# Quantizing the rotated y of a feed-forward stage: from token-major with transposes of z to channel-major, with maxima and factors carried by TensorE

## The reference, cut to what matters

```
def act_quant(x):                      # per token
    scale = 127.0 / clip(max(abs(x), axis=-1), 1e-5)
    return clip(round(x * scale), -128, 127) / scale

def h_bitlinear(x, w):
    xq = act_quant(fwht(x))            # Walsh-Hadamard transform along the channels
    return einsum('bsh,oh->bso', xq, weight_quant(w))    # weights -1, 0, 1 times a scale

gate = h_bitlinear(x, w_gate)          # 512 -> 2048
up   = h_bitlinear(x, w_up)            # 512 -> 2048
out  = h_bitlinear(silu(gate) * up, w_down)              # 2048 -> 512
```

## Time and profile before

| | |
|---|---|
| median of 3 runs | 3168.82 us (3165.68 to 3171.07) |
| the profiled execution's own time | 3169.14 us |
| its span | 3166.6 us |
| busy, share of the span | TensorE 87%, weight loads 46%, VectorE 63%, ScalarE 45%, GpSimd 32% |
| the feed-forward stage's loop | from about 2571.6 to 3077.2 us, 26 turns |

### The profile page before, as it was taken

How to read it: one execution, slowest core, us unless ns; L and a number is a source line. 1 busy time by engine, 2 the same in 40 slices (tenths; PEclk the granted TensorE clock), 3 DMA queues, 4 the chain that set the end, 5 groups by cost and what they waited for, 6 DMA issues and landing times. The chain is left out here.

```text
span 3166.6 us, 66615 instructions
## 1 busy us (share of the span) xinstructions
PE 2769.1 (87%) x26934; PEld 1468.4 (46%) x26968; DVE 1992.6 (63%) x2992; ACT 1438.4 (45%) x2378; POOL 1009.6 (32%) x712
## 2 busy tenths in 40 slices
PE   6999999387888888988845899999999799999997
PEld 2444444142444444444423444444444366666664
DVE  3444444359889898898891544445443377777776
ACT  2222222275667767757622422222222255666664
POOL 0000000108438347265390000000000077777776
PEclk9999999687898989889866999999999899999998
DMA  6999898300000000000002232322220101111110
GB/s 233 334 334 328 287 325 313 113 6 9 2 29 2 29 13 18 28 9 22 15 15 94 85 107 80 107 93 81 79 80 27 61 31 40 40 43 40 40 43 30
DMA packets 126427, 290.25 MB, mean 92 GB/s; under 512 B 30496, under 2 KB 35360, under 8 KB 122112
## 3 DMA queue, kind: packets, MB, share of 16 engines
q1 hardware_dynamic: 122752, 261.91, 23.7%
q10 hardware_dynamic: 3456, 25.17, 2.4%
HBM read 245.02 MB, written 42.01 MB: 91 GB/s over the span
## 5 line engine op out<-in xcount | busy, mean ns | idle before, releaser
L814 POOL TENSOR_TENSOR b_tmp<-b_L,b_U 128x496 f32<-128x496 f32 (+30 forms) x248 | 253.3, 1021 | 501.9 <-ACT b_L L1058 483.0
L2020 POOL TENSOR_TENSOR d_zb<-d_za 128x1024 f32<-128x1024 f32 x32 | 75.4, 2355 | 1007.6 <-DVE d_za L2082 1007.6
L860 PE MATMUL b_e<-b_hT,b_wqkv 128*128 128x512 f16 x1152 | 284.0, 393 | 46.4 <-DVE b_raw L1250 36.3
L1300 DVE TENSOR_TENSOR b_U<-b_U,b_tmp 128x1488 f32<-128x1488 f32 (+30 forms) x248 | 282.5, 1139 | 8.6
L816 POOL TENSOR_TENSOR b_U<-b_U,b_tmp 128x496 f32<-128x496 f32 (+30 forms) x248 | 274.3, 1106 | 19.4
L1298 DVE TENSOR_TENSOR b_tmp<-b_L,b_U 128x1488 f32<-128x1488 f32 (+30 forms) x248 | 264.9, 1068 | 17.4 <-ACT b_L L1058 11.8
L1526 PE MATMUL c_r<-c_hT,c_g_pair 128*128 128x512 f16 x1056 | 253.5, 392 | 13.1 <-DVE c_hT L1691 13.1
L1700 DVE SCALAR_TENSOR_TENSOR c_av<-c_r,c_sg 128x512 f32<-128x512 f32 x88 | 60.8, 691 | 303.0 <-PE c_r L1526 246.4
L1887 PE MATMUL d_m<-s_region,d_xiT 128*128 128x512 bf16 x1021 | 237.5, 384 | 6.2 <-ACT d_xiT L2000 2.2
L1526 PE MATMUL c_r<-c_hT,c_u_pair 128*128 128x512 f16 x1056 | 242.7, 379 | 0.0
L1526 PE MATMUL c_d<-c_d_pair,c_aT 128*128 128x512 f16 x1056 | 241.0, 379 | 0.0
(11 more groups left out here) (236 smaller groups left out, 5524.8 us busy)
## 6 DMA issues: line engine op xcount, KB each, us to landing
a_cT<-in_ctxT SPq DMA_DIRECT2D x128, 512.0 KB, 9.7
a_cn<-in_ctx SPq DMA_DIRECT2D x128, 512.0 KB, 8.9
a_x_ln<-in_x SPq DMA_DIRECT2D x8, 1024.0 KB, 16.2
a_cw<-in_ctx SPq DMA_DIRECT2D x128, 64.0 KB, 9.5
a_x_res<-in_x SPq DMA_DIRECT2D x32, 256.0 KB, 10.8
x<-a_x_out SPq DMA_DIRECT2D x32, 256.0 KB, 10.7
b_xg<-x SPq DMA_DIRECT2D x8, 1024.0 KB, 5.5
om<-b_hT SPq DMA_DIRECT2D x32, 256.0 KB, 2.0
```

The lines of the kernel that those rows point to most:

```text
L814: nc.gpsimd.tensor_tensor(tmp[:, QV, s + 1:S, :], lo, us, ALU.mult).then_inc(pool_prod, 1)
L860: mm = pe.matmul(p[:], w_qkv[:, a, i, n, c * P:(c + 1) * P], hp[:, b, n, :], start=(n + a + b == 0), stop=(n == DC - 1 and a == 1))
L1300: V.tensor_tensor(U[:, 0:QV, s + 1:S, :], U[:, 0:QV, s + 1:S, :], tmp[:, 0:QV, s + 1:S, :], ALU.subtract).then_inc(sub, 1)
L2020: nc.gpsimd.tensor_tensor(o[:, :, 0, :], a[:, :, 0, :], a[:, :, 1, :], ALU.add).then_inc(bf, 1)
```

## The change: what it does, and the diff

`rotate_y` swaps the operands: `had1` is stationary, and the four transposed chunks, 512 columns, are streamed. z comes out with channels on the partitions and (chunk, token) along the free axis, which is the form that the down projection wants, so the 16 transposes of z, their copies and the tile `zq` go.

Tokens now lie on the free axis, so the factor has to be found and applied otherwise:
- VectorE takes, for each channel-in-chunk and token, the largest magnitude over the 16 chunks (`largest`: `zm`, 128 x 128, read through a view whose inner step is 128 elements).
- TensorE transposes `zm` (`turn_largest`, between the gates 1 and 2), and VectorE reduces it to one number per token, from which the factor is worked out as before, and made a diagonal matrix (`factor`, after the second y).
- TensorE multiplies a matrix of ones with the diagonal (`spread_factor`, after the gates), which puts each token's factor on all partitions, and VectorE multiplies z with it, 2 x 1024 elements (`scaled`, after the fourth y).
- ScalarE adds the large constant and takes it off again in two passes for each half (`whole_z`), the second writing `ziT` in bf16. The clip goes.

The ring `RQ` now holds `largest`, `factor`, `down` and `pad`. `largest` and `down` share a bank, so the transpose of `zm` waits for `d_x_out`. GpSimd's last level waits for the product instead of ScalarE's passes.

```
-                    for c in range(4):
-                        mm = pe.matmul(p[:, c * P:(c + 1) * P], yT[:, 4 * j + c, :], had1, start=True, stop=True)
-                    mm.then_inc(full, 1)
+                    pe.matmul(p[:], had1, yT[:, 4 * j:4 * j + 4, :].rearrange("p c n -> p (c n)"),
+                              start=True, stop=True).then_inc(full, 1)
...
+            def turn_largest(i):
+                p, full = RQ.open(pe, i, "largest")
+                pe.wait_ge(zm_ready, i + 1)
+                pe.transpose(p[:, 0:P], zm[:], ident[:]).then_inc(full, 1)
+
+            def spread_factor(i):
+                p, full = RQ.open(pe, i, "factor")
+                pe.wait_ge(diag_ready, i + 1)
+                pe.matmul(p[:, 0:P], ones[:], diag[:], start=True, stop=True).then_inc(full, 1)
...
+            def whole_z(i, h):
+                act.wait_ge(zs_ready, 2 * i + h + 1)
+                half = slice(h * W // 2, (h + 1) * W // 2)
+                A.activation(zs[:, half], zs[:, half], ACT.Identity, bias=offset[:, 0:1]).then_inc(whole, 1)
+                act.wait_ge(whole, 2 * i + h + 1)
+                if h == 0 and not (isinstance(i, int) and i == 0):
+                    RQ.take(act, i - 1, "down")
+                part = ziT[:, WC // 2 * h:WC // 2 * (h + 1), :]
+                A.activation(part.rearrange("p c n -> p (c n)"), zs[:, half], ACT.Identity, bias=offset[:, 1:2])\
+                    .then_inc(zi_ready, 1)
...
+            def scaled(i):
+                dve.wait_ge(zi_ready, 2 * i)
+                p, free = RQ.take(dve, i, "factor")
+                for h in range(2):
+                    half = slice(h * W // 2, (h + 1) * W // 2)
+                    ins = V.tensor_tensor(zs[:, half].rearrange("p (c n) -> p c n", n=P),
+                                          z[:, half].rearrange("p (c n) -> p c n", n=P),
+                                          p[:, 0:P].unsqueeze(1).to_broadcast([P, WC // 2, P]), ALU.mult)
+                    ins.then_inc(zs_ready, 1)
+                dve.wait_ge(zs_ready, 2 * i + 2)
+                dve.sem_inc(free, 1)
...
+            def largest(i):
                 dve.wait_ge(bf, 6 * (i + 1))
-                V.tensor_reduce(amax2[:], z[:], AXX, ALU.max, apply_absolute_value=True).then_inc(am2, 1)
+                V.tensor_reduce(zm[:], z[:].rearrange("p (c n) -> p n c", n=P), AXX, ALU.max,
+                                apply_absolute_value=True).then_inc(zm_ready, 1)
+
+            def factor(i):
+                p, free = RQ.take(dve, i, "largest")
+                V.tensor_reduce(amax2[:], p[:, 0:P], AXX, ALU.max).then_inc(am2, 1)
                 dve.wait_ge(am2, 3 * i + 1)
+                dve.sem_inc(free, 1)
...
+                dve.wait_ge(q2, i + 1)
+                V.tensor_scalar(diag[:], ident[:], fac2[:, 0:1], None, ALU.mult).then_inc(diag_ready, 1)
```

More of the change, by code:

```diff
@@ L1805, in ffn_phase @@
         za, zb, z, zs = (sb(n, [P, W]) for n in ("za", "zb", "z", "zs"))
-        zq = sb("zq", [P, W], BF16)
+        zm, diag, ones = (sb(n, [P, P]) for n in ("zm", "diag", "ones"))
         amax2, step2, inv2, fac2, dsc = (sb(n, [P, 1]) for n in ("amax2", "step2", "inv2", "fac2", "dsc"))
@@ L1812, in ffn_phase @@
                   [f"z{j}" for j in range(NB)], 4, "m")
-        RQ = Ring(st, ["zi0", "zi1", "down", "pad"], 2, "q")
+        RQ = Ring(st, ["largest", "factor", "down", "pad"], 2, "q")
         set_ready = sem("set")
@@ L1816, in ffn_phase @@
         xT_hi, am, q1, xs_ready, clip1 = (sem(n) for n in ("xT_hi", "am", "q1", "xs_ready", "clip1"))
-        y_ready, zo_ready, first, bf, am2, q2, zs_ready, clip2 = (
-            sem(n) for n in ("y_ready", "zo_ready", "first", "bf", "am2", "q2", "zs_ready", "clip2"))
+        y_ready, zo_ready, first, bf, am2, q2, zs_ready = (
+            sem(n) for n in ("y_ready", "zo_ready", "first", "bf", "am2", "q2", "zs_ready"))
         dsc_ready, summed = sem("dsc"), sem("summed")
+        zm_ready, diag_ready, whole, zi_ready = (sem(n) for n in ("zm_ready", "diag_ready", "whole", "zi_ready"))
         def steps(eng, body):
@@ L1879, in transpose_xi, with gates @@
                 mm.then_inc(full, 1)
-            def gates(i, r):
-                RX.used(pe, r - 1, "xiT")
-                for j in range(NB):
+            def gates(i, r, js):
+                if js[0] == 0:
+                    RX.used(pe, r - 1, "xiT")
+                for j in js:
                     for n, w in (("g", w_g), ("u", w_u)):
@@ L1927, in body @@
                 if do["main"]:
-                    gates(k, r)
+                    gates(k, r, (0, 1))
+                if do["end"]:
+                    turn_largest(k - 2)
+                if do["main"]:
+                    gates(k, r, (2, 3))
+                if do["end"]:
+                    spread_factor(k - 2)
                 if do["one"]:
@@ L1938, in body @@
                     transpose_y(k)
-                if do["end"]:
-                    transpose_zi(k - 2, 0)
                 if do["main"]:
[L1942 to L1946, removed]
+                    rotate_y(k, range(NB))
                 if do["one"]:
@@ L1984, in body @@
                         A.copy(yT[:, 4 * j:4 * j + 4, :].rearrange("p c n -> p (c n)"), p[:]).then_inc(free, 1)
+                if do["end"]:
+                    whole_z(i, 0)
                 if do["one"]:
@@ L1989, in body @@
                 for h in range(2):
[L1990 to L1993, removed]
+                    if do["end"] and h == 0:
+                        whole_z(i, 1)
                     if do["main"]:
@@ L2029, in _ @@
             V = nc.vector
-            V.memset(offset[:], MAGIC).then_inc(set_ready, 1)
+            V.memset(offset[:, 0:1], MAGIC)
+            V.memset(offset[:, 1:2], -MAGIC).then_inc(set_ready, 1)
+            V.memset(ones[:], 1.0).then_inc(set_ready, 1)
             V.tensor_copy(ident16[:], ident[:]).then_inc(set_ready, 1)
@@ L2115, in body @@
                         gated(k, j)
-                    if do["end"] and j == 2:
-                        clip_z(i, 0)
+                    if do["end"] and j == 1:
+                        factor(i)
+                        V.tensor_scalar(dsc[:], step2[:], wscale[:, 2:3], 1.0 / QMAX, ALU.mult, ALU.mult)\
+                            .then_inc(dsc_ready, 1)
+                if do["end"]:
+                    scaled(i)
                 if do["two"]:
                     low_xT(k + 2, r)
-                if do["end"]:
-                    clip_z(i, 1)
                 if do["one"]:
```

33 lines of the change are left out of this document (5 added, 28 removed).

## The result

The changed kernel takes 3299.9 us (median of 4 runs, 3296.94 to 3302.22), the kernel before beside it 3167.25 (3163.13 to 3171.07): a ratio of 1.0419, 95% interval 1.0401 to 1.0437. The forecast was 3263 with a range up to 3300. The profiled execution took 3300.22, its span 3298.4 us.

The account below looks back on a forecast made before the run. TensorE bounds the kernel at 19.44 us a turn; the new loop of waits takes 21.81 plus 0.8 for the clock, 3.17 more over 29 intervals, 92 us, plus 2 at the end: 3169 + 94 = 3263 us, range 3200 to 3300.

Parts of the forecast that it names:

- closed row: Feed-forward loop: waits from ScalarE's `d_xT` to the next close a loop of 18.51 + R us, 21.81 a turn, over TensorE's 18.49.
- ScalarE's pairs: ScalarE between y's copies and `d_zo`: two dependent pairs of added passes, 2.04 us a pair, 4.08 a turn.
- my own case: Whole kernel: the stride costs VectorE time and the clock falls now and then; 3240 to 3290 us, chance 0.55.
- the list: Start-to-start steps of one turn across ScalarE, VectorE and TensorE, 21.81 us in sum, plus 0.8 for the clock.
- R: VectorE's strided reduction over z: its time, taken as 3.3 us, the middle between 2.29 and 4.28.
- 5.57 + 0.64 + 0.8: TensorE: `zm` transpose, gates, spread and rotation of x 5.57 us; x's transposes until `d_xT` 0.64; clock 0.8.
- The clock: TensorE behind the new gap: granted clock falls, costing 1.58 us, in half of the turns, so 0.8 a turn.
- A small reduction, a diagonal, all off the chain: VectorE's added products, small reduction and diagonal were to be off the chain; the products about 1.22 us each.
- The new wait: TensorE idles 2.3 us at the transpose of `zm`, whose bank `d_x_out` frees behind VectorE's strided reduction.
- One sign: Expected in the profile after: ScalarE's `d_zo` 4 us later behind y's copies than in the kernel before.
- TensorE's 18.49: TensorE's work in a turn of the changed loop without waits: 18.49 us, against 19.44 a turn before.
- Rival 3: Feed-forward loop: TensorE stays the bound, a turn is 0.95 us shorter, 3141 us in all; chance 0.05.

Follow-up runs that it names:

- Experiments 1: Changed kernel with the reduction over z reading 16 neighbours contiguously, the maxima taken over other elements: 3226.76 us, 1.0181 of the kernel before.
- experiment 4: Changed kernel with ScalarE's second pair of passes moved behind both `d_zo` and the copy of xi: 3237.22 us, 1.0218 of the kernel before.
- experiment 2: Changed kernel with 11 unused matmuls of 384 columns on TensorE ahead of the wait for `zm`: 3291.47 us, 1.0395 of the kernel before.
- experiment 5: Changed kernel with the diagonal written by ScalarE between its second and third silu, not by VectorE: 3260.85 us, 1.0292 of the kernel before.
- experiment 3: Changed kernel with maxima and down projection on separate banks and `d_x_out` behind the factor: 3296.59 us, 1.0397 of the kernel before.
- experiment 9: Version with passes and down projection one turn later and diagonal by ScalarE, its silus, passes and bank pad reordered: 3147.94 us, 0.9934 of the kernel before.
- experiment 7: Changed kernel with passes and down projection one turn later, z in two buffers, other banks, diagonal by ScalarE: 3185.69 us, 1.0058 of the kernel before.
- experiment 10: Changed kernel with VectorE's diagonal as a three-operand SCALAR_TENSOR_TENSOR in place of TENSOR_SCALAR: 3300.04 us, 1.0411 of the kernel before.

## Why the prediction was right, and where its terms were off

- **The mechanism** was the one forecast: a closed row through ScalarE's pairs, butterfly, reduction, `d_x_out`, gates and x's transposes, longer than TensorE's own work. Experiments 1 and 4 took one member each out, and the turn fell by nearly its length (4) or by more (1). Nearly all of the loss is in these turns: from the first reduction to the last are 598.7 us before and 727.8 after, 129 of 131 us. Behind the last one are 4.1 us more, forecast 2, and ahead of the first 1.3 less.
- **That the range held is luck.** 3299.9 is 0.1 us inside its end, with single runs on either side (3296.94 to 3302.22), and above the 3240 to 3290 of my own case. The kernel became 133 us slower, forecast 94.
- **The sum was short by 1.45 us a turn.** Along the list, from `d_xT` at 2824.06 to the next at 2848.12 are 24.06, forecast 21.81 + 0.8. The pairs took 2.37 and 2.22, not 2.04 twice: +0.51; a pass took 1.14 to 1.19, not the 1.06 of the earlier trace rows. From reduction to TensorE's transpose 4.54, not R + 1.00 = 4.30: +0.24. From the transpose to `d_xT` 7.78 in this turn, one with a fall of the clock, not 5.57 + 0.64 + 0.8: +0.77. The rest agrees within 0.07 in sum. The mean turn is 23.94, so 1.33 short, and 29 of these are 39 us: all that the forecast lacks. The row taken for a pass, line 1082 of the kernel, is a silu without a bias operand, the new passes have one; whether that makes the 0.1 us, no run shows.
- **R** is 3.69 in this turn. My 3.3, a middle between 2.29 and 4.28, was too low. The Trainium skill's figure ("Vector Engine (DVE) Microarchitecture Reference", section "Measured stream behaviour on trn2"), by which I had given an estimated 3.6 to 3.7, agrees with the trace. The single-source case that the same section reports at the full rate, a stream that alternates between two regions, did not carry over to this reduction.
- **The clock** fell in 17 of 26 turns, forecast half of them, and cost TensorE 1.4 to 1.7 us each time, forecast 1.58. But experiment 2 shows what that was worth to the turn: 0.34 us on average, forecast 0.8.
- **"A small reduction, a diagonal, all off the chain"** is the step that failed. From `d_x_out` there are two routes to the spread of the factor: TensorE's gates, at full clock 4.6 us (0.93 to the transpose, 0.2 for it, 3.46), and VectorE's y, y, factor, diagonal, 5.44 (2839.41 to 2844.85). The second is the longer one once the clock is whole. An error of 1 us here stood beside one on the clock with the other sign. The diagonal was long because of GpSimd: 0.40 us by ScalarE (experiment 5) gave 1.0 us a turn.
- **The new wait** was at the place forecast, 2.0 to 2.5 us (forecast 2.3), released by `d_x_out`. But taking the shared bank away gave nothing (experiment 3), because the diagonal held the spread at the same place; the bank is not shown to cost anything by itself.
- **One sign failed.** `d_zo` was to start 4 us later behind y's copies. It starts 7.15 us behind the first of them (2824.56 to 2831.71), before 4.91 (2815.58 to 2820.49), so 2.24 later: in the earlier trace rows a copy of `ziT` and 1.29 us of waiting stood in the pairs' place. The list itself had it right. Silu no longer waits for `d_fac`, as forecast.
- **TensorE's 18.49** and the rotation in 3.60 (forecast 3.61) held; experiment 9 runs at it. Rival 3, TensorE as the bound and 3141 us, is what that version comes near (3148), with the passes among the silus, where the prediction had said that they cost nothing.

## What to carry to other kernels

Work moved from an idle stretch of an engine to one that closes a loop between engines costs nearly its whole length (1.94 of 2.22 us a turn in experiment 4), though the engine's busy time hardly changes (in the loop's 26 turns ScalarE was busy 307.45 us before and 306.74 after). Two routes that run beside each other hide each other's cost: taking away one (the clock in experiment 2, the bank in experiment 3) shows next to nothing, and tells only that there is another. A small VectorE instruction beside GpSimd's work is as long as GpSimd leaves it: look at where it ends, not only at its length. When a change shortens the bound engine's work but lengthens such a loop, putting the tail a turn later is worth trying before tuning its members: here one pair moved gave 63 us (experiment 4), the later tail with its other changes 152 (experiment 9).

## What the hardware showed that I had not expected

- VectorE instructions of 128 or 512 columns with all their tensors in SBUF ended with GpSimd's running instruction: the diagonal 0.08 us after it in each turn of the loop, `d_xq` 0.28 after it in experiment 5. The diagonal took 0.29 us at least, 1.41 in the median and up to 2.01, in experiment 3 up to 2.43; `d_xq` took 0.43 in the median in experiment 7 and 1.48 in experiment 5. The kernel before had it too: its `d_zq` passes (line 2065, 1024 columns) took 1.1 and 2.1 us in the loop and 0.69 at the end, where GpSimd was done. Products with a PSUM operand (y 0.75, `d_zs` 1.22 in experiment 7), the reduction of z (2.29 without the stride) and one-column instructions (0.15) kept their length beside GpSimd's work. Which property decides was not settled; one source or two was not it (experiment 10).
- The length of the gap alone does not say whether the clock falls: behind a gap of 1.95 us (2600.10) 16 gate matmuls took 5.30, behind one of 2.35 (2768.94) 3.62. With gaps of 0.6 to 1.6 the loop's clock was 1.00 (experiments 1 and 4). The fall was seen over whatever stood behind the gap, gates or down projection.
- A maximum over 16 elements 512 bytes apart: 1.4 us more than over neighbours on 2048 elements, 0.69 ns each; 128 results in place of one cost nothing.
